# The rounded weights of the second int8 linear: made by POOL instead of ACT

## The reference, cut to what matters

```
x_q = clip(round(xs / x_scale), -127, 127)
w_q = clip(round(ws / w_scale), -127, 127)
return x_q @ w_q.T * x_scale * w_scale.T
```

## Time and profile before

| | us |
|---|---|
| Median of 3 executions | 468.9 (467.15 to 469.79) |
| The profiled execution | 467.85 |
| Its span in the profile | 466.1 |
| PE busy | 417.3 (90%) |
| DVE busy | 380.3 (82%) |
| ACT busy | 351.0 (75%) |
| POOL busy | 221.7 (48%) |

### The profile page before, as it was taken

One profiled execution on the slowest core, in us unless ns is written; L12 is line 12 of the kernel. 1 busy time (PEld: TensorE's weight loads), 2 busy tenths in 40 slices (PEclk: granted clock), 3 DMA queues, 4 the chain that ended last, 5 costly groups with the idle time before them and its releaser, 6 DMA issues.

```text
span 466.1 us, 7368 instructions
## 1 busy us (share of the span) xinstructions
PE 417.3 (90%) x2183; PEld 243.1 (52%) x2183; DVE 380.3 (82%) x955; ACT 351.0 (75%) x574; POOL 221.7 (48%) x343
## 2 busy tenths in 40 slices
PE   4738779987989987789999999999999999999986
PEld 3637557645746543345445545545544554554563
DVE  3797697989887889387898898889889889888853
ACT  1398887976799989857887787778788778777532
POOL 3277662689787754653333334434333333441220
PEclk9967989999999999999999999999999999999999
DMA  8999784653564701411231341232123123122101
GB/s 303 388 342 300 129 324 90 203 170 68 102 210 113 210 3 34 80 34 23 47 64 33 64 80 33 59 69 45 47 68 49 46 65 80 33 61 68 45 25 45
DMA packets 84952, 49.53 MB, mean 106 GB/s; under 512 B 70952, under 2 KB 73512, under 8 KB 83888
## 3 DMA queue, kind: packets, MB, share of 16 engines
q1 hardware_dynamic: 84912, 49.06, 39.6%
HBM read 28.33 MB, written 4.19 MB: 70 GB/s over the span
## 4 chain that ended last, share of the span: by engine, by line
PE 64%; DVE 9%; DMA 6%; POOL 6%; ACT 6%; issue 4%; SPq 3%; ACTq 0%; DVEq 0%; POOLq 0%
PE p_out L1901 11%; PE p_gate L1806 11%; PE p_out L1813 11%; PE p_val L1806 11%; PE p_tr L1788 3%; PE p_out L1835 3%; PE p_out L1861 3%; DMA att_t<-in_L_ffn_val_w 2%; SPq L414 2%; DMA att_t<-in_L_ffn_gate_w 2%; POOL w_slots L533 2%; PE p_gate L1735 2%; PE p_tr L1691 1%; ACT o_q L1291 1%; DVE h_max L779 1%
## 5 line engine op out<-in xcount | busy, mean ns | idle before, releaser
L1806 PE MATMUL p_gate<-gate_t,q_room 128*128 128x512 fp8e4 x256 | 65.7, 379 | 2.5 <-ACT p_gate L1406 2.5
L1806 PE MATMUL p_val<-val_t,q_room 128*128 128x512 fp8e4 x256 | 65.7, 379 | 0.2 <-ACT p_val L1416 0.2
L1813 PE MATMUL p_out<-att_t,qT_room 128*128 128x512 f32 x120 | 55.4, 603 | 0.9 <-ACT qT_room L1234 0.9
L1901 PE MATMUL p_out<-out_t,ws_f 128*128 128x512 fp8e4 x240 | 54.4, 379 | 0.9 <-DMA ws_f<-ws_f 0.9
L601 POOL TENSOR_TENSOR rstd<-mv,ln_eps 128x1 f32<-128x1 f32 x48 | 9.2, 191 | 93.9 <-DVE mv L870 86.8
L1406 ACT ACTIVATE p_gate<-w_slots,seed_scale 128x512 f32<-128x512 f32 x64 | 43.6, 684 | 11.3 <-POOL seed_scale L622 9.9
L1391 ACT ACTIVATE ctx_sb<-p_gate,bcol 128x512 f32<-128x512 f32 x64 | 43.8, 684 | 9.9 <-issue 4.5
L899 DVE TENSOR_TENSOR act_f<-p_val,ctx_sb 128x512 f32<-128x512 f32 x64 | 44.1, 689 | 6.8 <-PE p_val L1806 5.3
L901 DVE TENSOR_REDUCE mu<-act_f 128x1 f32<-128x512 f32 x64 | 43.9, 686 | 2.2
L1416 ACT ACTIVATE p_val<-w_in,seed_scale 128x512 f32<-128x512 f32 x64 | 43.5, 681 | 0.0
L1806 PEld LDWEIGHTS p_gate<-gate_t,q_room 128*128 128x128 f16 x256 | 24.9, 98 | 31.5 <-issue 8.6
(11 more groups left out here) (245 smaller groups left out, 983.1 us busy)
## 6 DMA issues: line engine op xcount, KB each, us to landing
att_t<-in_L_ffn_out_w SPq DMA_DIRECT2D x6, 1024.0 KB, 5.2
x_all<-in_x SPq DMA_DIRECT2D x4, 1024.0 KB, 14.5
att_t<-in_L_ffn_gate_w SPq DMA_DIRECT2D x4, 1024.0 KB, 13.1
att_t<-in_L_ffn_val_w SPq DMA_DIRECT2D x4, 1024.0 KB, 8.2
out_dram<-x_all SPq DMA_DIRECT2D x15, 256.0 KB, 2.3
w_in<-in_fside_BxS2xS SPq DMA_DIRECT2D x3, 1024.0 KB, 7.6
ctx_sb<-in_ctx SPq DMA_DIRECT2D x4, 512.0 KB, 6.3
out_t<-in_fside_BxS2xS SPq DMA_DIRECT2D x1, 1024.0 KB, 14.6
```

Of the source, the lines that this page charges most:

```text
L1806: last = nc.tensor.matmul(bank[:, c % 2, :], x_t[n % 2][:, k * P:(k + 1) * P], w_t[m][:, k, cols], start=False, stop=k == KD - 1, skip_gro ...
L1813: last = nc.tensor.matmul(p_out[:, 0, :], lt_c[:, k * P:(k + 1) * P], att_t[:, bass.ds((n // T) * (KD * S) + k * S, S)], start=k == 0, sto ...
L1901: last = nc.tensor.matmul(p_out[:, 0, :], p_t[:, k * P:(k + 1) * P], w_t[2][:, k, :], start=k == 0, stop=k == KH - 1)
```

## The change

The four roundings of the scaled weights of the o linear go from ACT to POOL, in each of the 4 batches: the calls `rounded(1, b, 1)` are gone from ACT's list, and POOL has `o_weights_rounded(b)` at four places of its list. A semaphore of its own, `o_w16`, counts them; `a_q16[1]` now counts the activations alone, 4 a batch instead of 8. All who waited for `a_q16[1]` wait for the one or the other with new counts: SP's transposes, DVE's `row_scales`, POOL's `scaled_weights` and `h_hidden`. The same data is waited for as before. The h linear is as it was.

```diff
+        def act_rounded(eng, z, batches):
+            need(eng, a_q16[z], T * (2 * batches - 1) if z == 0 else T * batches)
+        def weights_rounded(eng, z, batches):
+            need(eng, *((a_q16[0], T * 2 * batches) if z == 0 else (o_w16, T * batches)))
...
-                        sp.wait_ge(a_q16[z], T * (2 * b + r) + (part + 1) * T // QT_PARTS[z])
+                        done = (part + 1) * T // QT_PARTS[z]
+                        if z == 0:
+                            sp.wait_ge(a_q16[0], T * (2 * b + r) + done)
+                        else:
+                            sp.wait_ge((a_q16[1], o_w16)[r], T * b + done)
...
+                def o_weights_rounded(b):
+                    pool.wait_ge(a_qscale[1], 2 * b + 2)
+                    if b == 0:
+                        pool.wait_ge(tern_tr, 2 * 4)
+                    need(pool, a_qT[1][1], 16 * QT_PARTS[1] * b)
+                    for t in range(T):
+                        cols = slice(t * C, (t + 1) * C)
+                        nc.gpsimd.tensor_scalar(o_q16[1][:, cols], ws_o[:, cols], qscale[1][:, 1, t:t + 1], None, ALU.mult).then_inc(o_w16, 1)
...
                 scaled_weights(0, 2)
+                o_weights_rounded(0)
                 h_hidden(1, 2)
...
                 scaled_weights(1, 1)
                 root(0, 3)
+                o_weights_rounded(1)
                 w_round(8)
...
                 scaled_weights(1, 2)
+                o_weights_rounded(2)
                 h_hidden(3, 0)
...
                 scaled_weights(1, 3)
+                o_weights_rounded(3)
                 q_bias(0)
...
                 t_context(1)
-                rounded(1, 0, 1)
                 t_query_key(1)
...
                 rounded(1, 1, 0)
-                rounded(1, 1, 1)
                 h_silu(2, 0)
```

More of the change, by code:

```diff
@@ L277, in flamingo_gated_kernel @@
             sem(n) for n in ("a_bn", "a_stats", "a_rstd", "a_act", "a_hidden", "a_silu", "a_x"))
+        o_w16 = sem("o_w16")
         a_pool_chain, h_act_scaled, o_act_scaled, o_ctx_max, o_wscale = (sem(n) for n in ("a_pool_chain", "h_act_scaled", "o_act_scaled", "o_ctx_max", "o_wscale"))
@@ L559, in scaled_weights @@
                     pool.wait_ge(a_rows_copied[z], b + 1)
-                    need(pool, a_q16[z], T * 2 * b)
+                    weights_rounded(pool, z, b)
                     if z == 1 and b == 0:
@@ L573, in h_hidden @@
                     if t == 0:
-                        need(pool, a_q16[1], T * (2 * b - 1))
+                        act_rounded(pool, 1, b)
                     if b == 0 and t == 0:
@@ L814, in row_scales @@
                         dve.wait_ge((h_act_scaled, o_act_scaled)[z], b + 1)
-                    need(dve, a_q16[z], T * (2 * (b - 1) + r + 1))
+                    (act_rounded, weights_rounded)[r](dve, z, b)
                     if r == 1:
@@ L1290, in rounded @@
                         cols = slice(t * width[z], (t + 1) * width[z])
-                        nc.scalar.activation(q16_of[z][r][:, cols], (ws_of[z] if r == 1 else act_of(z, b))[:, cols], ACT.Copy,
+                        nc.scalar.activation(q16_of[z][r][:, cols], (ws_of[0] if r == 1 else act_of(z, b))[:, cols], ACT.Copy,
                                              scale=qscale[z][:, r, t:t + 1]).then_inc(a_q16[z], 1)
@@ L1545, in _ @@
                 rounded(1, 2, 0)
-                rounded(1, 2, 1)
                 t_query_key(3)
@@ L1578, in _ @@
                 rounded(1, 3, 0)
-                rounded(1, 3, 1)
                 b_gate(1, 2)
```

## The result

The changed kernel takes 482.5 us (median of 4, 480.06 to 484.11), the one before 468.0 (median of 4, 465.90 to 469.79). The ratio is 1.030, 95% interval 1.026 to 1.034: slower by 14.4 us where 7.6 were forecast. The direction was right; the size was not, and the time lies above the range.

What follows compares the result with a forecast made beforehand. The prediction took PE to bound the tile loop, so only the loop's start could move, set by hand-overs before it. Terms 4.4 + 2.1 + 1.1 = 7.6 us gave 476 against the median of 468.9; range 472 to 479.5.

Steps and rivals of the forecast that it cites:

- The price, 0.57 us: One 128x256 rounding on POOL: about 0.57 us each, 2.3 us for four, bounded by 0.38 and 0.73.
- 6.4 at 0.38: Rival on all batches: POOL's roundings are short, 0.38 us each, 6.4 us more, so 474.3; chance 0.08.
- dear: Rival: POOL's roundings cost 0.73 each or hold DVE; 9.2 us more, 477, up to 479.3; chance 0.12.
- Batch 0, +4.4: Batch 0: rounding queued behind `scaled_weights(0, 2)` on POOL, so PE starts at 102.4 instead of 97.94, 4.4 us later.
- Clock, +2.1: Batch 0: PE's clock falls after its idle stretch of 4.8 us, slowing products and energies by 2.1 us.
- Batch 1, +1.1: Batch 1: roundings push `w_round(8)` by 1.7; after a 0.81 us wait gives way and 0.2 for DVE, 1.1 us.
- the clock stays up: Rival: PE's clock does not fall, leaving 4.4 + 1.1, so 473.4 to 474.4; chance 0.18.
- Batch 2, "hidden": Batch 2: `h_hidden(3, 0)` 1.2 late, covered by DVE's 0.76 wait and `neg_max`'s slack; taken as 0, 0.4 without that slack.
- Batch 3, "hidden, no gain": Batch 3: weights come in time for SP's back-to-back transposes; no loss, and ACT's 1.6 us earlier end buys nothing.
- Caught up later: Rival: batch 0's delay is caught up in waits between 103 and 200 us; 1.5 to 4 us left; chance 0.08.
- faster: Rival: tile loop's start hangs on ACT, batch 0's delay is covered, 1.6 us come off: 466.3; chance 0.04.

Runs made afterwards that it cites:

- probe: Changed kernel with 14 groups of POOL tensor_scalar variants repeated behind its end; only group means are read: 921 ns for the change's form, 478 with a second factor.
- two_op: Changed kernel with a second factor 1.0 in POOL's four roundings per batch, same results; ratio to before 1.0123, +5.8 us.
- early0: Changed kernel with batch 0's rounding ahead of `scaled_weights(0, 2)` on POOL instead of behind it; ratio to before 1.0154, about 7 us below the change.
- clock0: Changed kernel with 24 extra matmuls of no use in PE's long pause of batch 0; ratio to before 1.0213, 4 us below the change.
- only1: Changed kernel with POOL rounding batch 1's weights alone, ACT those of the other batches; ratio to before 1.0050, +2.3 us.
- only3: Changed kernel with POOL rounding batch 3's weights alone, ACT those of the other batches; ratio to before 0.9993, -0.3 us.
- only2: Changed kernel with POOL rounding batch 2's weights alone, ACT those of the other batches; ratio to before 1.0069, +3.2 us.

## Why the forecast was right in kind and wrong in size

The forecast was 7.6 us more, in a range of 472 to 479.5; measured were 482.5 and 14.4 more.

**The price, 0.57 us (bounds 0.38 to 0.73): the step that failed most.** It measured 0.94 in the kernel and 0.92 on an idle machine, outside the bounds. The rows it was read from, the two tensor_scalar ones and the two-input one of the earlier trace rows, all do two operations or read two inputs. A one-operation tensor_scalar with an f32 input is in none of the rows, and I bounded it as if it could only be cheaper. The probe and two_op show that the form is the cause: 0.48 with a second factor, and +5.8 us (6.7 by the landmarks) in place of +14.4. At that price my working, between its 6.4 at 0.38 and 7.6 at 0.57, would have said 7.0. At 0.92, by my estimate, its terms come to 5.2 + 2.1 + 2.5 + 1.8 + 0.4 = 12.0: the price is 4.4 of the 7 us that were missing, and the waits and the clock below are the rest.

The rate of the Trainium skill (GPSIMD Engine Reference, section 3.1: 1.8 cycles per element at best, at 1.2 GHz; 0.38 us here by my estimate) fits neither form. Both have a fixed part of 0.26 to 0.28 us; the slope of the one-operation form is 2.5 ns a column, 3.0 cycles of that clock, and that of the two-operation form 0.84 ns, 1.0 cycle.

Of the rivals, "dear" had the sign and the mechanisms, but stopped at 0.73.

**Batch 0, +4.4: 5.3.** The chain was as told: rounding behind `scaled_weights(0, 2)`, first pair, landing 4.1 later, PE. With 0.92 in place of the working's 0.57 it gives 97.00 + 1.84 + 4.1 = 102.9 for the landing, 103.1 for PE, hence 5.2. early0 shows that the place makes it.

**Clock, +2.1: 2.7 in batch 0, and some 1.2 in batch 1.** The granted clock was 0.50 from behind the pause to about 109, and clock0 gives the same 3.38 us as before for that stretch at full clock. The rival "the clock stays up" falls. The second stretch, in batch 1 (0.53 at 137 to 139), wasn't forecast; what it cost is in the next paragraph.

**Batch 1, +1.1: 3.5 in the changed kernel, 2.3 measured alone.** The push of `w_round(8)` was forecast at 1.7, and 3.1 by the price that was measured (124.7 in place of 121.59); it is 11.0 late after 8.0. Against it I set a 0.81 us wait of POOL for DVE's `rz_att` at 139.65. It gave nothing back: `w_transpose(11)` is 11.4 late. What took the credit away is the clock. `rz_att` is released by ACT's `e_att`; ACT comes there without a pause from its copy of what PE's `t_query_key(2)` made, and had waited 0.97 us for that. PE's `w_transpose(8)` is 10.0 late. From there to the end of `t_query_key(2)` PE ran at half clock in part, and that end is 11.5 late, as `rz_att` is.

Early0 bears this out. It has the same roundings, and in batch 1 the same waits of PE for `w_slots` and of DVE for `a_f`, but the clock stays at 1.00:

```profile
129.08 1.07 PE L1686 MATMUL p_val<-ident,w_slots 128*128 128x128 f16 x16 [1.96 <-POOL w_slots L545]
...
132.27 1.44 DVE L857 SCALAR_TENSOR_TENSOR side<-p_gate,scale,side 128x512 f32<-128x512 f32 x2 [3.75 <-POOL a_f L589]
```

There the credit was paid as forecast: `w_round(8)` is 5.5 late, `w_transpose(11)` 4.7; in two_op 6.5 and 5.7. In the two other traces with a fall in batch 1 it was not: 3.2 and 3.6 in only1, 8.4 and 8.8 in clock0. So the term was right but for the price, and a fall of the clock that I hadn't reckoned with took the 0.8 us and 0.4 more. Why the clock fell in some and not in early0, behind the same 1.96 us wait, is open.

**Batch 2, "hidden": 2.3, and 3.2 alone.** This is the second step that failed: a wait put at nothing. It fails on `gate_marks()`, which I hadn't put into the chain. The 0.76 us taken for cover was a wait for work that hangs on the same delay.

**Batch 3, "hidden, no gain": right.** only3 is 0.9993, no gain and no loss that can be told; in the changed kernel 0.8 us were lost there by the landmarks. ACT's relief does reach PE there: the 0.99 us that PE waited for ACT's `att_t` ahead of `t_energies(3, 2)` are gone. But PE waits them away at the transposes, 2.51 us in place of 0.95. ACT is busy 5.9 us less, and no landmark is earlier.

**Caught up later, or faster: both rivals fall.** From the first `c_attend` on, the changed kernel keeps its 14.6 us to the end (14.8). The batches measured alone sum to 13.3 us, and by their landmarks to more: 8.4 for batch 0, 3.9, 4.3 and 0.5 for the others, 17.1 against 14.8. Most of this excess, 1.6 us, is the fall of the clock in the trace of only2, which that of the changed kernel doesn't have.

**What stays open.** The landmarks of only1 and only2 show 1.1 to 1.6 us more than the timed runs. Each trace has one fall of the clock worth about that, and the mean granted clock of their ten executions runs from 0.978 to 0.989 and from 0.975 to 0.985, so others may lack it; that is argued, not shown. Open is also what makes a fall, since it comes in one execution and not in the next, and how much two_op would gain with the clock held through the whole preparation: both experiments on it had a fall in batch 3.

## What to carry to other kernels

Price an instruction by a row of its own form, number of operations included: the same POOL scaling cost 0.92 us with one operation and 0.48 with two. A wait counts as cover only if what it waits for doesn't hang on the delay that it is to hide; follow the releaser one step further, past the engine, before calling it slack. Before a delay is put down to a wait, look whether the clock was the same: here one credit of 0.8 us was paid at full clock and lost in the three traces in which the clock fell at that place. And where an engine's list is full of hand-overs, ask of an inserted instruction which of the next three behind it somebody waits for: moving it behind the first found the second.

## What the runs showed of the hardware

- POOL's tensor_scalar, f32 in, f16 or f32 out: one operation 921, 1564 and 2843 ns at 128x256, x512 and x1024; two operations 478, 695 and 1121 ns. A number instead of a pointer makes the one-operation form 846 to 849 ns. The value of the data (scaled weights or activations, factors 1.0, 1e-6 or 0.0) makes no difference over 3 ns.
- A pause of PE of 5.64 us was followed by some 6 us at the granted clock of 0.50, 1.2 GHz. Bridged with 48 matmul records in 5.52 us, the clock stayed at 1.00 in batch 0.
- A pause of 1.96 us in batch 1 was followed by 3 to 4 us at 0.50 in the changed kernel, only1 and clock0, and by none in early0.
- One stretch at 0.50 near 70 us, there in eight traces and missing in seven, makes 1.5 us of difference between executions of the same code.
- A DVE instruction of 0.17 us took 1.76 us under POOL's running row and ended within 0.03 us of a POOL instruction; one of the kernel before took 1.25 us in the same way.
